# Four graph layers in one kernel: another copy and product order in the edge loops of layers 2 and 3, narrower node products, other scatter shares

## The chip, the cores and the metric

The kernel runs on one core of one Trainium2 chip. The metric is the device time of one execution in microseconds. Engines are called PE (matrix products), DVE, ACT, POOL and SP; each takes its own list of instructions in order and waits on semaphores (counters) for the others. PEld is the loading of a product's stationary operand, which overlaps PE. DMAs are issued from the queues of SP, ACT and POOL.

## What is computed

Four layers of message passing (l = 0 to 3) over N = 6250 nodes with 160 features each (64 scalars and 32 vectors of three) and E = 100000 edges. Each layer adds to the node features. The reference, cut to the pattern of one layer (l = 0; the others differ in widths, in the activation, and l = 2 also has a cross product and gates its output):

```python
h = jnp.maximum(_layernorm(x, axis=-1), 0.0)
x0, x1 = _split(h)                                   # 64, 32x3
s0, s1 = _fctp_scalar_attr(x0, x1, z, W_sc0, W_sc1)  # skip rows
h0, h1 = _fctp_scalar_attr(x0, x1, z, W_l1_0, W_l1_1)
w = jax.nn.silu(edge_features @ W_fc1 / np.sqrt(NEF)) @ W_fc2 / np.sqrt(RN)
...
e0, e1 = h0[edge_src], h1[edge_src]
m0a = w0 * e0 * y0
m0b = w3 * jnp.einsum('eui,ei->eu', e1, y1) / np.sqrt(3.0)
m1a = (w1 * e0)[:, :, None] * y1[:, None, :]
m1b = w2[:, :, None] * (e1 * y0[:, :, None])
ns = jax.ops.segment_sum(mid_s, edge_dst, num_segments=N) * inv
nv = jax.ops.segment_sum(mid_v, edge_dst, num_segments=N) * inv
o0, o1 = _fctp_scalar_attr(ns, nv, z, W_l2_0, W_l2_1)
...
x = x + jnp.concatenate([c_s * s0 + c_x * o0, (c_s * s1 + c_x * o1).reshape(N, -1)], axis=1)
```

The last layer weighs skip rows and sums with the cosine and sine of an angle, itself a product of the sums.

## The kernel before

**Data.** Nodes lie in NB = 51 tiles of BN = 123. Edges are sorted by the tile of the node that they add to and padded, so that a group of GE = 512 edges (G = 4 columns of 128 partitions) adds to one tile; there are 208 groups in a layer, as 26 rounds of the loop variable i with eight groups u each. Edge tables TA (36 columns, for l = 0, 1, 3) and TB (72 columns, l = 2) lie in DRAM. TB is built by POOL, by indirect DMAs that scatter rows (L566): 2 x 200 of its 782 columns inside the edge loops of l = 0 and 1, the rest in three shares, BCH[0] of 174 columns before l = 0 and two of 104 between l = 0 and 1 and between 1 and 2.

**An edge stage** (one per layer) works group by group, two groups (u, u + 1) to a step, and the order on each engine is written out by hand:
- SP loads the group's table rows (L459, `load`).
- POOL gathers the node rows HT of the source nodes, four indirect DMAs a group (L647, `gather`).
- PE transposes the edge features (`tfeat`, L829, L834, L839), ACT copies them out (`edge_e`, L1058, L1060, L1062), PE multiplies by the first weights (`edge_f1`, called F1, L850, L854, L857), ACT applies the activation (`edge_s`, L1072, L1075), PE multiplies by the second weights (`edge_f2`, F2, L867, L872).
- DVE builds the one-hot matrix OH (L1538) and the messages from F2's result and the gathered rows (L1547 to L1568; for l = 2 L1575 to L1600), the last of which raises semaphore M. In l = 2 ACT makes a copy of two of three products for the cross product (L1091); in every layer it makes twelve scalings (L1096, `edge_n`, semaphore N).
- PE multiplies the messages with OH (`edge_a`, A, L884), and DVE adds the result to the tile's sums ACC (L1509, semaphore V).

PE's order for a pair of groups is F1(u+2), F1(u+3), F2(u+2), A(u), transposes (u+4), (u+5), F2(u+3), A(u+1) (L907 to L914). ACT's is the two feature copies (u+2), (u+3), then scalings and activations in turn (L1101 to L1111). For l other than 2, DVE also splits the features of a later group into three bf16 parts in a ring XS of four buffers, four groups ahead (`parts`). Semaphores M and N of a layer start at 4 (L1317, L947), so that a loop's first rounds wait on positive numbers.

**A node stage** is `phase(lo, ln)` on every engine: it ends layer lo and begins layer ln, 51 tiles in turn. PE: the output product `mout` of the sums (L781), then, LAG = 10 tiles later, transposes (`tnode`, L735 to L740) and node linear (`mnode`, L751 to L761). ACT: normalised rows (`hid_`, L965), copying out the linear (`evac`, L976), clearing the sums (`clear`, L996), and the stores of HT and of the skip rows SC (`store`, L383, L386; for ln = 3 these are issued by SP). DVE: the new x (L1414) and the statistics of its layer norm. `mout` has nch = 3 products (4 for l = 2), one for each chunk of 128 (120) rows of the sums, all with the full output width: 160, 320 (as 2 x 160), 192 and 161 columns. Many of these columns have only zero weights for a given chunk. The node linear of l = 2 is four products.

After the last edge loop `phase(3, None)` computes the angles and the outputs, and puts them out in waves of tiles, LASTB.

## Time and profile before

| | |
|---|---|
| median of 3 runs | 5998.29 us (5996.16 to 6000.24) |
| the profiled execution | 5996.94 us, span 5994.8 us |
| PE busy | 4832.2 us, 81% of the span |
| PE weight loads | 4213.6 us, 70% |
| DVE busy | 4676.4 us, 78% |
| POOL busy | 4130.4 us, 69% |
| ACT busy | 3728.3 us, 62% |
| mean granted clock of PE | 0.953 |

The stages, as cut from the timeline, in us from the start of the span: preparation and the nodes of l = 0 to 453; edges of l = 0 to 1768; nodes 0 to 1 until 1903; edges of l = 1 to 3226; nodes 1 to 2 until 3422; edges of l = 2 to 4648; nodes 2 to 3 until 4855; edges of l = 3 to 5912; the last outputs to 5995. A busy share says how much of the time an engine had work, not that its work set the pace. The list of waits gives, for an engine and line, the idle time ahead of it and the instruction whose end is taken to have released it; "issue" there means idle time without a visible wait. An ended wait costs time only where the engine's next work is what the rest waits for.

### The profile page before, as it was taken

Reading aid. Unit: us, or ns where it says so; the run is one execution under the profiler, and the core shown is the slowest. Engines: PE = TensorE matmul, PEld = TensorE weight load, DVE = VectorE, ACT = ScalarE, POOL = GpSimd, SP = SyncE. Lnnn points to the kernel's source line nnn. Section 1 sums busy time; section 2 is a strip of 40 time slices with the busy share of each in tenths; the row PEclk is TensorE's granted clock in tenths of the full one; section 3 lists DMA queues with packets and bytes.
Section 4 is the critical chain, followed back from the end, with each engine's and each line's share of the span. In section 5 each row is a group of like instructions: output and inputs, shape, how many; then the busy total and the mean of one; then the engine's idle time right before and its main releaser. Section 6 shows DMA issues by size and latency. Waiting matters only on the chain. (4 is left out here: it accounts for less than half of the span.)

```text
span 5994.8 us, 143106 instructions
## 1 busy us (share of the span) xinstructions
PE 4832.2 (81%) x37237; PEld 4213.6 (70%) x37237; DVE 4676.4 (78%) x14209; ACT 3728.3 (62%) x12996; POOL 4130.4 (69%) x4263
## 2 busy tenths in 40 slices
PE   0078787777888888888889899999999778888886
PEld 0047777777777777777777688888888657777776
DVE  9947777777777777777776499999998569999996
ACT  0046666666665666666665477777777567777774
POOL 1677777777777777777777377777776257777773
PEclk9999999999998999999999899999999879999998
DMA  6433333333333333333333233333333223333332
GB/s 196 112 83 73 75 75 75 75 76 75 75 81 80 75 75 75 76 75 75 74 82 76 81 81 82 81 80 82 81 81 73 73 71 84 83 84 84 82 79 63
DMA packets 599359, 487.97 MB, mean 81 GB/s; under 512 B 308216, under 2 KB 525558, under 8 KB 598871
## 3 DMA queue, kind: packets, MB, share of 16 engines
q0 software_dynamic: 195056, 322.11, 21.0%
q1 hardware_dynamic: 365562, 137.46, 10.1%
q10 hardware_dynamic: 38637, 27.25, 1.5%
q8 instruction: 37, 0.61, 0.0%
q14 instruction: 67, 0.55, 0.0%
HBM read 410.36 MB, written 75.56 MB: 81 GB/s over the span
## 5 line engine op out<-in xcount | busy, mean ns | idle before, releaser
L884 PE MATMUL PS<-WK 128*128 128x123 f32 (+1 forms) x21632 | 2714.0, 285 | 196.8 <-issue 190.0
L884 PEld LDWEIGHTS PS<-WK 128*128 128x128 f32 (+1 forms) x21632 | 2598.1, 198 | 357.9 <-issue 349.2
L1096 ACT ACTIVATE WK<-WK 128x64 f32<-128x64 f32 x9984 | 2468.7, 334 | 352.1 <-DVE WK L1550 351.5
L647 POOL DMA_INDIRECT WK<-HT,WK x2080 | 2032.4, 977 | 797.7 <-issue 706.6
L647 POOL DMA_INDIRECT ACC<-HT,WK x832 | 795.8, 957 | 253.4 <-issue 242.7
L566 POOL DMA_INDIRECT TB<-WK x718 | 720.1, 1003 | 248.3 <-issue 230.7
L1072 ACT ACTIVATE WK<-PS 100x512 f32<-100x512 f32 x420 | 247.0, 588 | 693.3 <-PE PS L850 693.2
L867 PE MATMUL PS<-F,WK 100*128 100x192 f32 x3360 | 657.6, 340 | 11.2 <-DVE WK L1568 8.8
L872 PE MATMUL PS<-F,WK 64*128 64x224 f32 (+1 forms) x3360 | 416.3, 367 | 214.6 <-ACT WK L1075 214.6
L867 PEld LDWEIGHTS PS<-F,WK 100*128 100x128 f32 x3360 | 541.4, 192 | 66.5 <-DVE WK L1568 37.4
L1538 DVE SCALAR_TENSOR_TENSOR WK<-iota,BKOA,WK 128x492 f32<-128x492 f32 x624 | 453.3, 726 | 156.8 <-PE PS L884 107.6
L647 POOL DMA_INDIRECT WOA<-HT,WK x416 | 435.6, 1047 | 172.9 <-issue 118.3
L872 PEld LDWEIGHTS PS<-F,WK 64*128 64x128 f32 x3360 | 280.6, 189 | 317.0 <-issue 305.3
L1547 DVE TENSOR_TENSOR WK<-WK 128x384 f32<-128x384 f32 x416 | 232.6, 559 | 343.5 <-DMA WK<-HT,WK 340.7
L1509 DVE TENSOR_TENSOR ACC<-ACC,PS 128x369 f32 (+1 forms) x832 | 474.5, 570 | 0.0
L1547 DVE TENSOR_TENSOR WK<-ACC,WK 128x384 f32<-128x384 f32 x208 | 116.2, 559 | 308.5 <-DMA ACC<-HT,WK 308.5
L1075 ACT ACTIVATE WK<-PS 64x256 f32<-64x256 f32 x840 | 316.1, 376 | 55.7 <-PE PS L854 45.4
L1058 ACT ACTIVATE WK<-PS 72x512 bf16<-72x512 bf16 (+1 forms) x420 | 225.6, 586 | 113.4 <-PE PS L829 108.6
L850 PE MATMUL PS<-WK,FB 72*100 72x512 bf16 (+1 forms) x420 | 166.8, 397 | 157.7 <-issue 152.7
L829 PE MATMUL PS<-identb,WK 128*72 128x128 bf16 (+1 forms) x1696 | 154.5, 223 | 150.9 <-DVE WK L1487 117.7
L1558 DVE TENSOR_TENSOR WK<-PS,WK 128x256 f32<-128x256 f32 x624 | 261.8, 420 | 0.0
L829 PEld LDWEIGHTS PS<-identb,WK 128*72 128x72 bf16 (+1 forms) x1696 | 114.7, 112 | 180.8 <-issue 168.6
(234 smaller groups left out, 6605.7 us busy)
## 6 DMA issues: line engine op xcount, KB each, us to landing
WK<-TA SPq DMA_DIRECT2D x636, 72.0 KB, 1.9
WK<-HT,WK POOLq DMA_INDIRECT x2080
WK<-TB SPq DMA_DIRECT2D x212, 144.0 KB
WK<-in_ea SPq DMA_DIRECT2D x23, 612.0 KB
TA<-WK POOLq DMA_DIRECT2D x23, 612.0 KB, 7.9
ACC<-HT,WK POOLq DMA_INDIRECT x832
WK<-in_eb SPq DMA_DIRECT2D x400, 32.0 KB
HT<-WK ACTq DMA_DIRECT2D x153, 76.9 KB
```

Of the source, the lines that this page charges most:

```text
L566: eng.indirect_dma_start(out=T[:, :], out_offset=bass.IndirectOffsetOnAxis(ap=ps(q), axis=0), in_=st[:, q, :], in_offset=None).then_inc(sm ...
L647: eng.indirect_dma_start(out=GB[l][u % 4][:, t, :], out_offset=None, in_=HT[:, :], in_offset=bass.IndirectOffsetOnAxis(ap=idx[:, t, vc:vc ...
L829: m = eng.transpose(psT[k][0:6 * kf_, t * 128:(t + 1) * 128], x[:, t, 0:6 * kf_], identb[:, :])
L867: m = eng.matmul(psW[q][:, t, 0:wn], HH[l][q][0:hid, t * 128:(t + 1) * 128], F2[l][:, :], start=True, stop=True)
L872: m = eng.matmul(psW[q][:, a // 32 + t, 0:wn], HH[l][q][a:a + 64, t * 128:(t + 1) * 128], F2[l][a:a + 64, :], start=True, stop=True)
L884: m = eng.matmul(psA[q][0:ch, k * BN:(k + 1) * BN], ms[:, t, k * ch:(k + 1) * ch], OH[q][:, t, :], start=(t == 0), stop=(t == G - 1))
L1075: m = eng.activation(hh[a:a + 64, 0:256], psQ[q][a // 64][a:a + 64, :], p["fn"], scale=p["scale"])
L1096: m = eng.activation(m4[:, t, 96 + vb * c:160 + vb * c], m4[:, t, 96:160] if l == 2 else TW[l][q][:, t, :], ACT.Copy, scale=tb[:, t, y1 + ...
L1509: eng.tensor_tensor(acc[:, bass.ds(j, 1), :], acc[:, bass.ds(j, 1), :], psA[q][0:ch, 0:na].unsqueeze(1), ALU.add).then_inc(e.V, 1)
L1538: op(eng.scalar_tensor_tensor(out=OH[q], in0=iota1[:, :].unsqueeze(1).to_broadcast([128, G, BN]), scalar=BKO[b][:, bass.ds(i * 8 + (u + 2) ...
L1547: kp = op(eng.tensor_tensor(tp[q], e1, y1b.to_broadcast([128, G, 3, 32]), ALU.mult))
L1558: op(eng.tensor_tensor(m4[:, :, 0:64], W[:, :, 0:64], ty, ALU.mult))
```

## The change

Layers count from 0 in the code; the "layer 3" of the change is l = 2 in the order of the edge loop (which l = 3 takes over as well), and l = 2 for the node linear.

- **Edge loops of l = 2 and 3.** Everything up to the activation runs two groups further ahead: PE's order for a pair becomes F2(u+2), A(u), F2(u+3), transposes (u+6), (u+7), F1(u+4), F1(u+5), A(u+1). ACT's becomes the copy for u (`edge_w`, l = 2), the activations (u+2), (u+3), the scalings of u, the copy for u + 1, the feature copies (u+4), (u+5), the scalings of u + 1. What opens and ends the loops follows. In l = 3 DVE splits features six groups ahead instead of four, and the table rows have one semaphore a group (`landed`) instead of one a pair. M and N start at 8.
- **Output products.** `fed(l, k)` gives the columns that the rows of chunk k feed; the products run over these alone. Chunk 0 comes first and covers all.
- **Node linear of l = 2.** Two products instead of four: the weights WS2 get 32 columns of zeros, and the results go to the same places with strides.
- **Scatters.** The shares become 166, 96 and 120 columns.

```diff
-SB0, SB1 = 174, 104
+SB0, SB1, SB2 = 166, 96, 120
 NT0 = 25
 HC = EC // 2
 SLOOP = NT0 * 8
 
 
 NMIN, NMAX = 26, 31
-assert SB0 + 2 * SLOOP + 2 * SB1 == EC and EC % CHA == 0
+assert SB0 + 2 * SLOOP + SB1 + SB2 == EC and EC % CHA == 0
 BLK, LAG = 4, 10
...
 
 
-BCH = [chunks(0, SB0), chunks(SB0 + SLOOP, SB1), chunks(SB0 + 2 * SLOOP + SB1, SB1)]
+BCH = [chunks(0, SB0), chunks(SB0 + SLOOP, SB1), chunks(SB0 + 2 * SLOOP + SB1, SB2)]
 BL0 = [SB0, SB0 + SLOOP + SB1]
...
-        WS = [sb("WS0", [64, 128]), sb("WS1", [128, 128]), sb("WS2", [64, 160]), sb("WS3", [64, 128])]
+        WS = [sb("WS0", [64, 128]), sb("WS1", [128, 128]), sb("WS2", [64, 192]), sb("WS3", [64, 128])]
...
+                self.one = l == 3
+                self.L = [sem(f"e{l}_L{i}") for i in range(8 if l == 3 else 4)]
                 self.G = [sem(f"e{l}_G{i}") for i in range(4)]
                 self.T, self.E, self.F1, self.S, self.F2, self.M, self.A, self.V, self.D, self.N = (
                     sem(f"e{l}_{n}") for n in ("T", "E", "F1", "S", "F2", "M", "A", "V", "D", "N"))
+
+            def landed(self, eng, g, i):
+                if self.one:
+                    eng.wait_ge(self.L[g % 8], i * 16 + 16 * (g // 8 + 1))
+                else:
+                    eng.wait_ge(self.L[g % 8 // 2], i * 32 + 32 * (g // 8 + 1))
...
             loads += [(RW[a], w[f"L1_gnn_Ws_l2_{s}"]), (RW[2 + a], w[f"L1_gnn_Wv_l2_{s}"])]
         loads += [(RW3s, w["L1_gnn_Ws_l3"]), (RW3v, w["L1_gnn_Wv_l3"])]
-        loads += [(WS[2][:, 0:64], w["L2_gnn_W_nl0"]), (WS[2][:, 64:160], w["L2_gnn_W_skip0"])]
+        loads += [(WS[2][:, 0:64], w["L2_gnn_W_nl0"]), (WS[2][:, 96:192], w["L2_gnn_W_skip0"])]
...
+        def fed(l, k):
+
+            p, ns = LAYERS[l], 96 if l == 2 else 64
+            if k == 0:
+                return 0, 161 if l == 3 else ns + 96
+            blocks = [(0, 96, 0, ns)] + [(96 + c * p["vb"], p["vb"], ns + 32 * c, 32) for c in range(3)]
+            hit = [(c, c + n) for f, m, c, n in blocks if f < (k + 1) * p["ch"] and k * p["ch"] < f + m]
+            return hit[0][0], hit[-1][1]
+
...
 
                 def load(i, u):
-                    k = i * 8 if i is n else i * 8 + (u - 3)
-                    eng.wait_ge(e.M, 4 if isinstance(i, int) else k)
-                    eng.wait_ge(e.N, 4 if isinstance(i, int) else k)
+                    k = i * 8 + (u + 1)
+                    eng.wait_ge(e.M, 8 if isinstance(i, int) else k)
+                    eng.wait_ge(e.N, 8 if isinstance(i, int) else k)
                     r = eng.value_load(TI[b][32:33, bass.ds(i * 8 + (u + 2), 1)], min_val=0, max_val=EPAD)
-                    eng.dma_start(TT[l][u], T[bass.ds(r, GE), :].rearrange("(p t) f -> p (t f)", t=G)).then_inc(e.L[u // 2], 16)
+                    eng.dma_start(TT[l][u], T[bass.ds(r, GE), :].rearrange("(p t) f -> p (t f)", t=G)).then_inc(e.L[u if l == 3 else u // 2], 16)
...
                     idx = TT[l][u].rearrange("p (t f) -> p t f", t=G)
-                    eng.wait_ge(e.L[u // 2], i * 32 + 32)
-                    eng.wait_ge(e.M, i * 8 + (u + 1))
+                    e.landed(eng, u, i)
+                    eng.wait_ge(e.M, i * 8 + (u + 5))
...
                     if ln == 2:
-                        eng.matmul(o[:, 0:64], t[0:64, 0, 0:BN], WS[2][:, 0:64], start=True, stop=True)
-                        eng.matmul(o[:, 160:256], t[0:64, 0, 0:BN], WS[2][:, 64:160], start=True, stop=True)
-                        eng.matmul(o[:, 64:160], t[0:96, 1, 0:BN], KV[2][:, 0:96], start=True, stop=True)
-                        m = eng.matmul(o[:, 256:352], t[0:96, 1, 0:BN], KV[2][:, 96:192], start=True, stop=True)
+                        s2 = o[:, 0:320].rearrange("p (a f) -> p a f", a=2)[:, :, 0:96]
+                        v2 = o[:, 64:448].rearrange("p (a f) -> p a f", a=2)[:, :, 0:96]
+                        eng.matmul(s2, t[0:64, 0, 0:BN], WS[2][:, :], start=True, stop=True)
+                        m = eng.matmul(v2, t[0:96, 1, 0:BN], KV[2][:, :], start=True, stop=True)
                     else:
                         v = o[:, 0:320].rearrange("p (a f) -> p a f", a=2)
...
                             eng.wait_ge(s_xo, base + j - 3)
-                    nc_ = WO[lo].shape[2]
                     for k in range(nch):
-                        m = eng.matmul(psO[j % 4][0:BN, 0:nc_], acc[:, j, k, :], WO[lo][:, k, :],
-                                       start=(k == 0), stop=(k == nch - 1))
+                        c0, c1 = fed(lo, k)
+                        if lo == 1:
+                            o = psO[j % 4][0:BN, 0:320].rearrange("p (a f) -> p a f", a=2)[:, :, c0:c1]
+                            w_ = WO[1][:, k, :].rearrange("p (a f) -> p a f", a=2)[:, :, c0:c1]
+                        else:
+                            o, w_ = psO[j % 4][0:BN, c0:c1], WO[lo][:, k, c0:c1]
+                        m = eng.matmul(o, acc[:, j, k, :], w_, start=(k == 0), stop=(k == nch - 1))
                     m.then_inc(s_oo, 1)
 
...
                     elif not isinstance(i, int):
                         eng.wait_ge(e.D, i * (8 * ND[l]) + (u + 1) * ND[l])
                     elif g == 0:
                         eng.wait_ge(s_xp, min(l, 2) + 1)
+                    elif g == 4:
+                        eng.wait_ge(s_xp, 4)
                     if not isinstance(i, int) or g >= 2:
                         eng.wait_ge(e.E, i * 8 + (g - k))
-                        if l >= 2:
-                            eng.wait_ge(e.S, i * 8 + (g - k))
+                    if l >= 2 and (not isinstance(i, int) or g >= 4):
+                        eng.wait_ge(e.S, i * 8 + (g - k - 2))
                     eng.sem_inc(s_sep, 1)
                     x = XS[g % 4]
...
                     eng.wait_ge(e.S, i * 8 + (g + 1))
-                    eng.wait_ge(e.M, i * 8 + (g + 3))
+                    eng.wait_ge(e.M, i * 8 + (g + 7))
                     if l < 2:
                         for t in range(G):
...
                     ms = MS[l][q][:, 0:G * nm].rearrange("p (t f) -> p t f", t=G)
-                    eng.wait_ge(e.M, i * 8 + (u + 5))
-                    eng.wait_ge(e.N, i * 8 + (u + 5))
+                    eng.wait_ge(e.M, i * 8 + (u + 9))
+                    eng.wait_ge(e.N, i * 8 + (u + 9))
                     eng.wait_ge(e.V, i * 8 + (u + 2))
                     for k in range(nch):
...
-                edge_f1(0, 0, 0)
-                edge_f1(0, 1, 0)
-                tfeat(0, 2, 0)
-                tfeat(0, 3, 0)
+                if l < 2:
+                    edge_f1(0, 0, 0)
+                    edge_f1(0, 1, 0)
+                    tfeat(0, 2, 0)
+                    tfeat(0, 3, 0)
+                else:
+                    tfeat(0, 2, 0)
+                    tfeat(0, 3, 0)
+                    edge_f1(0, 0, 0)
+                    edge_f1(0, 1, 0)
+                    tfeat(0, 4, 0)
+                    tfeat(0, 5, 0)
+                    edge_f1(0, 2, 0)
+                    edge_f1(0, 3, 0)
                 edge_f2(0, 0, 0)
                 edge_f2(0, 1, 0)
 
...
-                        edge_f1(i, u, 2)
-                        edge_f1(i, u + 1, 2)
-                        edge_f2(i, u, 2)
-                        edge_a(i, u)
-                        tfeat(i, u, 4)
-                        tfeat(i, u + 1, 4)
-                        edge_f2(i, u + 1, 2)
-                        edge_a(i, u + 1)
-
-                eng.wait_ge(e.T, n * 8 + 4)
-                eng.wait_ge(e.F1, n * 8 + 2)
+                        if l < 2:
+                            edge_f1(i, u, 2)
+                            edge_f1(i, u + 1, 2)
+                            edge_f2(i, u, 2)
+                            edge_a(i, u)
+                            tfeat(i, u, 4)
+                            tfeat(i, u + 1, 4)
+                            edge_f2(i, u + 1, 2)
+                            edge_a(i, u + 1)
+                        else:
+                            edge_f2(i, u, 2)
+                            edge_a(i, u)
+                            edge_f2(i, u + 1, 2)
+                            tfeat(i, u, 6)
+                            tfeat(i, u + 1, 6)
+                            edge_f1(i, u, 4)
+                            edge_f1(i, u + 1, 4)
+                            edge_a(i, u + 1)
+
+                o = 2 if l >= 2 else 0
+                eng.wait_ge(e.T, n * 8 + (4 + o))
+                eng.wait_ge(e.F1, n * 8 + (2 + o))
...
-                    eng.wait_ge(e.F1, i * 8 + (g + 1))
+                    eng.wait_ge(e.F1, i * 8 + (g + 1 if l < 2 else g - q + 2))
                     if not (isinstance(i, int) and g < 2):
                         eng.wait_ge(e.F2, i * 8 + (g - 1))
...
-                edge_s(0, 0, 0)
-                edge_s(0, 0, 1)
+                if l < 2:
+                    edge_s(0, 0, 0)
+                    edge_s(0, 0, 1)
+                else:
+                    edge_s(0, 0, 0)
+                    edge_s(0, 0, 1)
+                    edge_e(0, 0, 2)
+                    edge_e(0, 0, 3)
+
+                def edge_w(i, u):
+
+                    eng.wait_ge(e.D, i * (8 * ND[l]) + (u * ND[l] + KW))
+                    eng.activation(tw[:, :, 3:5, :], tw[:, :, 0:2, :], ACT.Copy).then_inc(s_tw, 1)
+
                 def edge_n(i, u):
 
                     q = u % 2
                     R, y1 = (RB, SHC) if l == 2 else (RA, YC + 1)
                     tb = TT[l][u].rearrange("p (t f) -> p t f", t=G)
                     m4 = MS[l][q][:, 0:G * (96 + 3 * vb)].rearrange("p (t f) -> p t f", t=G)
-                    if l == 2:
-
-                        eng.wait_ge(e.D, i * (8 * ND[l]) + (u * ND[l] + KW))
-                        eng.activation(tw[:, :, 3:5, :], tw[:, :, 0:2, :], ACT.Copy).then_inc(s_tw, 1)
-                    else:
-                        eng.wait_ge(e.D, i * (8 * ND[l]) + (u * ND[l] + KT))
+                    eng.wait_ge(e.D, i * (8 * ND[l]) + (u * ND[l] + KT))
                     for t in range(G):
                         for c in (1, 2, 0):
...
-                        edge_e(i, u, 2)
-                        edge_e(i, u + 1, 2)
-                        if l >= 2:
+                        if l < 2:
+                            edge_e(i, u, 2)
+                            edge_e(i, u + 1, 2)
+                            edge_s(i, u, 2)
                             edge_n(i, u)
-                        edge_s(i, u, 2)
-                        if l < 2:
+                            edge_s(i, u + 1, 2)
+                        else:
+                            if l == 2:
+                                edge_w(i, u)
+                            edge_s(i, u, 2)
+                            edge_s(i, u + 1, 2)
                             edge_n(i, u)
-                        edge_s(i, u + 1, 2)
+                            if l == 2:
+                                edge_w(i, u + 1)
+                            edge_e(i, u, 4)
+                            edge_e(i, u + 1, 4)
                         edge_n(i, u + 1)
                 eng.wait_ge(s_le, l + 1)
 
...
                         w_()
-                    for u in range(4):
-                        eng.wait_ge(e.L[u // 2], 32)
+                    for u in range(4 if l < 2 else 6):
+                        if u == 4:
+                            eng.sem_inc(s_xp, 1)
+                        if u >= 4:
+                            eng.wait_ge(e.T, u - 3)
+                        e.landed(eng, u, 0)
                         x0, x1, x2 = parts(u)
                         for x in (x0, x1) + x2:
...
                             y0 = tb[:, :, yc:yc + 1]
-                            u4 = (u + 4) % 8
-                            x0, x1, x2 = parts(u4)
+                            ahead = 4 if l < 2 else 6
+                            x0, x1, x2 = parts((u + ahead) % 8)
                             kp = op(eng.tensor_tensor(tp[q], e1, y1b.to_broadcast([128, G, 3, 32]), ALU.mult))
                             eng.wait_ge(e.F2, i * 8 + (u + 1))
-                            eng.wait_ge(e.N, i * 8 + (u + 3))
+                            eng.wait_ge(e.N, i * 8 + (u + 7))
                             kt = op(eng.tensor_tensor(TW[l][q], W[:, :, 64:128], e0, ALU.mult))
                             assert kt == KT
...
-                            eng.wait_ge(e.L[u4 // 2], i * 32 + (32 * ((u + 4) // 8) + 32))
-                            eng.wait_ge(e.T, i * 8 + (u + 1))
+                            e.landed(eng, u + ahead, i)
+                            eng.wait_ge(e.T, i * 8 + (u + ahead - 3))
                             k0 = op(x0())
                             need(kr)
```

(The remaining lines move starting values and counts of semaphores with these: `sem_inc(EG[ln].M, 8)`, `sem_inc(EG[ln].N, 8)`, waits on M and N four higher, and some semaphores of the preparation that are merged into one.)

## Rows read from the trace of the kernel before

**Rows 1.** Windows by stage: us, busy (count) of PE, PEld, DVE, ACT, POOL; clock; DMA share; GB/s.
```profile
1768.00:1903.00 135.00, 119.26 (x800) 111.01 (x801) 105.22 (x463) 68.78 (x174) 98.01 (x100) 0.92 0.37 86
1808.00:1828.00 20.00, 20.00 (x145) 19.14 (x145) 18.59 (x84) 10.02 (x27) 15.43 (x16) 1.00 0.43 101
3226.00:3422.00 196.00, 177.73 (x873) 129.14 (x874) 81.78 (x346) 77.32 (x176) 92.85 (x98) 0.87 0.32 85
3422.00:4648.00 1226.00, 1165.98 (x10820) 1001.78 (x10818) 1128.19 (x2498) 907.98 (x3326) 863.01 (x824) 1.00 0.31 80
4648.00:4855.00 207.00, 147.77 (x748) 123.55 (x750) 97.52 (x465) 97.45 (x201) 50.19 (x66) 0.78 0.26 70
4855.00:5912.00 1057.00, 898.60 (x7912) 781.68 (x7910) 955.27 (x3121) 832.44 (x3118) 788.77 (x824) 0.96 0.34 81
```

**Rows 2.** Waits, 3422 to 4648 us: engine, line <- releaser: us, times, longest.
```profile
PE PS L872 <- ACT WK L1075: 58.5, 104, 5.8
```

**Rows 3.** Timeline, l = 2: start, us, engine, line, operation, [idle before <- releaser].
```profile
4011.80 3.65 PE L884 MATMUL PS<-WK 128*120 128x123 f32 x32
4015.38 1.08 PE L854 MATMUL PS<-WK,F 64*64 64x256 f32 x8
4016.97 1.03 PE L872 MATMUL PS<-F,WK 64*128 64x224 f32 x8 [0.51 <-ACT WK L1075]
...
4021.51 1.09 PE L834 MATMUL PS<-ident,WK 128*64 128x128 f32 x16
4022.53 1.03 PE L872 MATMUL PS<-F,WK 64*128 64x224 f32 x8
...
4015.59 0.73 DVE L1538 SCALAR_TENSOR_TENSOR WK<-iota,BKOB,WK 128x492 f32<-128x492 f32 x1
...
4019.89 0.55 DVE L1600 TENSOR_TENSOR WK<-WK 128x384 f32<-128x384 f32 x1
...
4016.07 1.56 ACT L1075 ACTIVATE WK<-PS 64x256 f32<-64x256 f32 x4 [0.42 <-PE PS L854]
4017.88 0.42 ACT L1091 ACTIVATE WK<-WK 128x256 f32<-128x256 f32 x1 [0.24 <-DVE WK L1580]
4018.20 2.96 ACT L1096 ACTIVATE WK<-WK 128x64 f32<-128x64 f32 x12
```

**Rows 4.** Waits, 4855 to 5912 us (the edge stage of l = 3).
```profile
POOL WK L647 <- issue: 231.8, 761, 0.3
...
POOL WK L647 <- PE PS L903: 3.1, 1, 3.1
```

**Rows 5.** Timeline, PE and its weight loads, between l = 0 and 1, then 1 and 2.
```profile
1802.87 0.98 PE L781 MATMUL PS<-WOA,ACC 128*123 128x160 f32 x6
...
3302.26 1.80 PE L781 MATMUL PS<-WOA,ACC 128*123 128x320 f32 x6
...
3304.20 0.29 PEld L751 LDWEIGHTS PS<-WS,WK 64*123 64x123 f32 x2 [0.17 <-issue]
...
3304.41 0.29 PEld L752 LDWEIGHTS PS<-WS,WK 64*123 64x123 f32 x2
...
3305.30 1.80 PE L781 MATMUL PS<-WOA,ACC 128*123 128x320 f32 x6
```

**Rows 6.** Timeline, stores being issued: ACT's queue from 1 to 2, SP's from 2 to 3.
```profile
3305.27 1.23 ACTq L383 DMA_DIRECT2D HT<-WK  x1
...
3306.53 1.91 ACTq L386 DMA_DIRECT2D SC<-WK  x1
...
4831.48 1.15 SPq L386 DMA_DIRECT2D SC<-WK  x1
```

**Rows 7.** Timeline, DVE in the last stage.
```profile
5921.17 0.17 DVE L1373 TENSOR_TENSOR ANG<-WK,ZZ 123x7 f32<-123x7 f32 x1 [8.40 <-ACT WK L1002]
```

**Rows 8.** Timeline, DVE before the first edge loop; waits, 3226 to 3422 us.
```profile
439.06 0.23 DVE L1484 CAST WK<-WK 128x144 bf16<-128x144 f32 x1 [16.90 <-ACT ACC L1043]
...
POOL WK L647 <- issue: 73.8, 8, 71.6
```

44 lines of the change are left out of this document (23 added, 21 removed).

## The prediction

> **What bounds the kernel now.** I read the stages first, since the whole-run shares (PE 81%, DVE 78%, POOL 69%) average over stages with different limits. Four edge stages (208 groups of 512 edges each) alternate with node stages. The first two edge loops get no changed instruction, so I read only the others [rows 1]. "l" counts layers from 0, so the change's "layer 3" is l = 2 and its neighbours.
>
> In the edge stage of l = 2 PE works 1166 of 1226 us, and the list of waits names one hole in it: the F2 product (L872) waits for ACT's activation (L1075) 104 times, 58.5 us in all, once per pair of groups [rows 1, 2]. In order of time, one pair on PE is: A 3.58 (11.80 to 15.38), F1 and its wait for ACT 1.59 (to 16.97), F2 0.96 and A 3.58 (together to 21.51), the transposes 1.02 (to 22.53), F2 0.96: 11.69 us [rows 3]. 104 such pairs are 1216 of the stage's 1226 us.
>
> In l = 3 the list of waits says something else: POOL pauses 0.30 us before nearly each gather and hardly for anything else [rows 4], and its 824 recorded instructions take 788.77/824 = 0.96 each [rows 1]. 832 gathers of 1.26 us are 1048 of 1057 us. That loop is bound by POOL's issuing.
>
> In the node stages PE is nearly always busy from l = 0 to 1 (20.00 of 20 us, with DVE at 18.59), and busy 178 of 196 us from 1 to 2, where a node takes 3.04 (3302.26 to 3305.30, from one L781 to the next) [rows 1, 5]. From 2 to 3 its mean clock is only 0.78 and other things end the waits [rows 1].
>
> **The change part by part.**
>
> *Narrower output products (L781).* Six instructions of 160 columns take 0.98 us and six of 320 take 1.80 [rows 5]: 0.82/(6 x 160) = 0.85 ns per column and instruction. A floor is seen beside it: two weight loads of 123 columns follow each other in 0.21 us although their products have only 64 columns, 0.105 each [rows 5]. So narrowing below about 123 columns buys nothing. Each product is two instructions. Layer 0 goes from 3 x 160 to 160, 64, 64: 4 x 37 x 0.85 ns = 0.13 us a node. Layer 1 from 3 x 320 to 320, 128, 128: 4 x 192 x 0.85 = 0.65. Layer 2 from 4 x 192 to 192, 64, 64, 32: 6 x 69 x 0.85 = 0.35. Layer 3 as layer 0. Times 51 nodes this is 7, 33, 18 and 7 us of PE.
>
> *Two products for the node linear of l = 2.* Four take 1.10 us (3304.20 to 3305.30) [rows 5]. Two of 192 columns are four instructions of 192 x 0.85 = 0.16 and two starts of about 0.15, 0.95 in all: 0.15 a node.
>
> What of this is on the path:
> - 0 to 1: DVE's 18.59 of 20 us allows 7% of some 80 us, so 6 at most where PE's share is 7. I take **-5** (bounds -7 and -2). POOL's scatters, shortened by 8 here, must end first; else they would be next.
> - 1 to 2: PE's 3.04 us a node become 2.24, but each node also has two stores issued from ACT's queue, and these take 1.23 and 1.91 us to issue while ACT's next work stands behind them [rows 6]: 3.1 us, as long as PE's node. This queue is late next. Without the row loads of SP, SP's stores of the next stage show 1.15 an issue, about 2.4 a node [rows 6]. The stage has 51 nodes; at 3.1 until the row loads end (about 60% of it) nothing is won, after that up to 0.6 a node, about 20 x 0.6 = 12, and about 4 in the first ten nodes, which have no stores. Against this the table loads of l = 2, which follow the scatters, come 16 x 1.26 = 20 us later (a scatter costs what a gather does: 92.85/98 = 0.95 busy [rows 1] and, as I take it, the same pause) and so into these last stores. I take **-5**, bounds +5 and -25 (all 51 nodes at 2.4).
> - 2 to 3: SP issues two stores a node, 2.4 us [rows 6], as long as PE's whole node now. PE's 18 us are hidden by them; only the start gains. **-1**, bounds -5 and +10.
> - The last stage: DVE idles 8.40 us until the first seven outputs are through [rows 7]; later it is DVE that has work. A quarter of these 8.40 goes: **-2**, bounds -4 and +10.
>
> *Scatters shared out anew.* 8 fewer before l = 0: DVE's wait there ends with ACT's clear of the accumulator (16.90 us of waiting for it [rows 8]), so 8 x 1.26 us of POOL's time gain **0**. If that cover were gone they would be worth 10. 16 more from 1 to 2 take 20 us of POOL, which idles 71.6 us there before its first gather [rows 8]: **0**.
>
> *The order in the edge loop of l = 2.* This is the large item on paper: F1 now runs a pair ahead, so the wait of 58.5 us for ACT cannot occur. What is late next? The new PE order is F2(u+2), A(u), F2(u+3), transposes (u+6, u+7), F1(u+4, u+5), A(u+1). F2(u+3) waits for DVE's messages of group u+1 (semaphore M), and behind it on PE now stand the transposes and F1, which before were done while DVE worked. That closes a loop: A(u-1) starts, DVE starts u+1 after it (4011.80 to 4015.59, 3.79 us), finishes its messages 4.85 us later (4020.44), then F2 0.96, transposes 1.02, F1, A(u+1) [rows 3]. F1 before another product is not in the trace: its eight instructions last 1.08, the transposes last 1.09 and give way after 1.02, so I take 1.01 (bounds 0.85 and 1.2). With 0.07 of signalling: 3.79 + 4.85 + 0.07 + 0.96 + 1.02 + 1.01 = **11.70 us a pair**, against 11.69 now. ACT closes a second loop: its two activations (1.56 together) now stand between the copy and the twelve scalings, so group u's scalings end 2.29 (the copy's start, 15.59 to 17.88) + 0.32 + 1.56 + 2.96 = 7.1 us after DVE starts u [rows 3], and A(u) waits for them. A(u), F2, transposes, F1 and A(u+1) until DVE may start u+3 add 3.58 + 0.96 + 1.02 + 1.01 + 3.79, the next group 5.5: 23.0 for two pairs, 11.5 each. Below the first, so it doesn't decide. Item: 104 x 0.01 = **+1**, bounds 104 x (11.54 - 11.69) = -16 and 104 x 0.2 = +21. PE alone would need 2 x 3.58 + 2 x 0.96 + 1.02 + 1.01 = 11.1, DVE 1128/104 = 10.85 [rows 1]; see the rival. The longer prologue (copy, F1 of groups 2 and 3 before F2 of group 0) delays the first group by about 2 us, of which the earlier first A gives back one: **+1**.
>
> *The same order in l = 3.* The gathers bound it. Its own loop as above is shorter than POOL's 8 x 1.26 = 10.1 a pair (A, F2 and F1 are shorter), and what PE no longer waits for falls on an engine with time to spare (busy 899 of 1057 us [rows 1]). Only the start changes, where POOL waits 3.1 us for the opening products [rows 4]: **-1**, bounds -4 and +3. The copy of 6 pieces ahead rather than 4 has its table rows loaded long before; landing by tile instead of by pair costs nothing.
>
> *Sum:* -5 - 5 - 1 - 2 + 0 + 1 + 1 - 1 = -12 us on the profiled execution's 5996.94 (span 5994.8 and 2.1 around it), 5985. The median of the runs is 1.35 us above that execution, within their spread. **Forecast 5985 us.**
>
> **The rivals.**
> - *The hole simply closes.* If PE, once rid of ACT, goes at its own 11.1 us a pair, l = 2 gains 104 x 0.55 = 57 us instead of losing 2: 5927. For it: PE is the busiest engine there. Against it: the first loop above is made of durations that stand in the rows, and nothing in the change takes its DVE part away.
> - *The stores don't bind from 1 to 2.* If the long issues are only the queue filling at PE's pace, the stage gains up to 25: 5965. For it: PE is busy 178 of the 196 us [rows 1]; against it: the two issues together are as long as the node, which needs no queue to explain it.
> - *The clock falls (slower).* From 2 to 3 the granted clock averages 0.78, and 1.00 in the dense 20 us of 0 to 1 [rows 1]; PE is given gaps by this change in each node stage. At 1.2 GHz a node of 1 to 2 costs PE about 4.1 us instead of 2.24, 1.0 more than today. It decides from the point where 13 nodes run so (13 us eat the gain); at half of the two middle stages it costs 27: 6012. The Trainium skill ("TensorE: Matmul & The Clock Gate", "Part 1: The HAM clock gate") has the array throttled by default and released by activity, so it speaks against thinning PE's work; by it alone this case would be the one to expect. The edge loops, which have gaps too, run at 0.96 and 1.00 [rows 1].
> - *Nothing is on the path:* the node stages wait for stores and DVE throughout, and l = 2 stays as it is: 5997.
>
> The Trainium skill ("DMA: Bandwidth & Descriptors", "Why a DMA increments its semaphore by 16 and not by 1") lets a transfer use as many engines as divide its row count, which for 123 rows is three; that fits the stores' long issues, which no row explains, and speaks for stores as the next bound.
>
> **How the numbers follow.** Forecast case 0.52, with its own range 5972 to 6000 (l = 2 from -16 to +21 in the main); closed hole 0.12; stores free 0.14; clock 0.14; nothing 0.08. A measurement of this kernel tells about 0.2%, 12 us, from no change. Of the forecast case 0.28 falls below 5986 and 0.24 inside 12 us; both gaining rivals count as faster, the clock as slower, the last as same: faster 0.54, same 0.32, slower 0.14. The range 5945 to 6010 leaves out most of the closed hole and about half of the clock case.
>
> **What would show it.** In l = 2: PE's wait for L1075 gone, in its place waits of L872 for DVE's L1600 and of L884 for ACT's L1096, the pair at 11.6 to 11.8. In l = 3: POOL still 1.26 a gather. From 1 to 2: L781 near 1.1 us for six, stores still 2.4 to 3.1 us a node. I am wrong if the pair of l = 2 falls under 11.4, if the stage from 1 to 2 shrinks by over 15 us, or if L781's weight loads go under 0.1 us apart.

## The result, and the profile after

The changed kernel takes **6036.14 us** (median of 4 runs, 6032.48 to 6038.70), the kernel before 5997.23 beside it: a ratio of 1.0062 with a 95% interval of 1.005 to 1.0075. It is 0.6% slower, where 5985 us and a gain were forecast, and it lies outside the range of 5945 to 6010. The profiled execution took 6038.70 us with a span of 6036.9.

The stages of both profiled executions, cut at the first output product and at the first opening product (L903, after the change L939) of each stage:

| stage | before, us | after, us | difference | forecast |
|---|---|---|---|---|
| preparation, nodes of l = 0 | 453.1 | 452.9 | -0.2 | 0 |
| edges l = 0 | 1315.2 | 1317.4 | +2.3 | 0 |
| nodes 0 to 1 | 134.2 | 130.4 | -3.8 | -5 |
| edges l = 1 | 1323.8 | 1328.6 | +4.8 | 0 |
| nodes 1 to 2 | 195.3 | 193.0 | -2.4 | -5 + 1 |
| edges l = 2 | 1227.1 | 1228.9 | +1.8 | +1 |
| **nodes 2 to 3** | 206.6 | 233.8 | **+27.2** | -1 |
| edges l = 3 | 1057.7 | 1052.2 | -5.5 | -1 |
| **last outputs** | 81.8 | 99.8 | **+18.0** | -2 |

Seven of nine stages came within 5 us of their terms, the edge loop of l = 2 with all its new order among them. The whole loss lies in two stages whose PE got less to do. The windows of those stages in the changed kernel, with columns as in [rows 1]: start and end; us; busy and count of PE, PEld, DVE, ACT, POOL; granted clock; DMA share; GB/s. A clock of 1.00 is 2.4 GHz, one of 0.50 is 1.2 GHz. The first line is the first 5 us of the stage.

```profile
4651.20:4656.20 5.00, 5.00 (x30) 5.00 (x31) 0.00 (x0) 1.11 (x1) 2.71 (x2) 0.72 0.17 48
...
4651.00:4885.00 234.00, 198.51 (x762) 165.40 (x762) 98.36 (x472) 100.46 (x203) 50.26 (x66) 0.51 0.23 62
4690.00:4720.00 30.00, 30.00 (x113) 25.40 (x112) 14.41 (x70) 15.74 (x32) 6.58 (x9) 0.50 0.25 65
4720.00:4860.00 140.00, 140.00 (x505) 114.50 (x503) 63.76 (x310) 67.99 (x138) 22.89 (x35) 0.50 0.22 63
...
5935.00:6036.00 101.00, 69.59 (x306) 69.44 (x306) 43.75 (x154) 16.21 (x56) 3.85 (x1) 0.51 0.18 51
```

The same places of the kernel before:

```profile
4648.70:4653.70 5.00, 4.99 (x31) 5.00 (x32) 0.00 (x0) 1.15 (x1) 2.68 (x2) 1.00 0.12 33
...
4690.00:4720.00 30.00, 30.00 (x170) 25.58 (x170) 21.43 (x105) 21.61 (x45) 8.61 (x13) 0.98 0.33 89
...
5912.00:5995.00 83.00, 43.92 (x306) 43.70 (x306) 43.30 (x153) 16.71 (x56) 3.85 (x1) 0.77 0.22 61
```

In both kernels PE is busy for all of the 30 us from 4690, but before it does 170 products there at a clock of 0.98, and after only 113 at 0.50, though each now has fewer columns. Then PE works 140 of 140 us without a gap at a clock of 0.50. In the last stage PE's 306 products take 69.6 us instead of 43.9.

Both kernels pause in this stage: after the first four nodes' output products PE waits 16 us for the skip rows, and the clock is 0.50 when it goes on. With the full width it comes back: in the kernel before it is 1.00 from 4694 to 4728 us, falls after a second pause at 4755 us and is 1.00 again by 4780. With the narrow products it does not come back in this stage. It is already lower ahead of the first pause, 0.72 against 1.00 in the first 5 us, in which PE is busy throughout in both kernels.

One node of the stage from 2 to 3 on PE, before and then after:

```profile
4710.50 0.27 PE L739 MATMUL PS<-ident,WK 123*64 123x123 f32 x1
...
4711.21 0.59 PE L763 MATMUL PS<-KV,WK 96*123 96x192 f32 x2
4711.64 1.47 PE L781 MATMUL PS<-WO,ACC 120*123 120x192 f32 x8
4712.94 0.27 PE L739 MATMUL PS<-ident,WK 123*64 123x123 f32 x1
```

```profile
4720.95 0.39 PE L759 MATMUL PS<-ident,WK 123*64 123x123 f32 x1
...
4722.20 1.00 PE L783 MATMUL PS<-KV,WK 96*123 96x192 f32 x2
4722.99 1.93 PE L806 MATMUL PS<-WO,ACC 120*123 120x192 f32 x8
4724.73 0.39 PE L759 MATMUL PS<-ident,WK 123*64 123x123 f32 x1
```

The operations that nobody changed show the clock: L783 is L763 of before and takes 1.00 instead of 0.59. The eight output products take 1.93 us instead of 1.47 in spite of 352 columns a pass instead of 768.

The Trainium skill ("TensorE: Matmul & The Clock Gate", "Part 1: The HAM clock gate") calls the throttled state the default, which activity releases. This trace agrees on the two levels (0.50 and 1.00), but not on "activity", if one reads that as PE having instructions: 140 us without a gap released nothing.

**The edge loop of l = 2** has the pair that was forecast. PE in the changed kernel:

```profile
4011.26 1.03 PE L898 MATMUL PS<-F,WK 64*128 64x224 f32 x8 [0.29 <-DVE WK L1665]
4012.21 1.09 PE L860 MATMUL PS<-ident,WK 128*64 128x128 f32 x16
4013.24 1.08 PE L880 MATMUL PS<-WK,F 64*64 64x256 f32 x8
4014.25 3.65 PE L910 MATMUL PS<-WK 128*120 128x123 f32 x32
4017.83 1.03 PE L898 MATMUL PS<-F,WK 64*128 64x224 f32 x8
4019.03 3.62 PE L910 MATMUL PS<-WK 128*120 128x123 f32 x32 [0.17 <-issue]
4022.95 1.03 PE L898 MATMUL PS<-F,WK 64*128 64x224 f32 x8 [0.30 <-DVE WK L1665]
```

From F2 (L898) at 4011.26 to F2 at 4022.95 is 11.69 us, as before [rows 3]; the product behind F1 (L880) starts 1.01 us after it. The waits of that stage (engine, line waited for, releaser: us, times, longest):

```profile
DVE WK L1603 <- PE PS L910: 91.7, 104, 3.4
...
PEld PS L898 <- DVE WK L1665: 50.1, 104, 6.2
...
PE PS L898 <- DVE WK L1665: 28.7, 79, 5.4
...
PE PS L910 <- ACT WK L1150: 9.9, 25, 0.6
```

The wait for L1075 [rows 2] is gone. In its place F2 or its weight load waits for DVE's last message (L1665) in every pair, and DVE waits for A to end (L910) in every pair: the loop that the forecast closed.

### The profile page after: what moved, and what is told of

It reads as the page before. It is cut to its first block and busy times, and to the rows that moved or that the text cites. A ratio compares the mean times of both kernels' runs of the same rounds, so it can differ in the third digit from the quotient of the medians.

```text
span 6036.9 us, 143521 instructions
## 1 busy us (share of the span) xinstructions
PE 4852.7 (80%) x37069; PEld 4220.0 (70%) x37069; DVE 4668.0 (77%) x14217; ACT 3745.6 (62%) x13000; POOL 4126.4 (68%) x4264
## 5 line engine op out<-in xcount | busy, mean ns | idle before, releaser
L910 PE MATMUL PS<-WK 128*128 128x123 f32 (+1 forms) x21632 | 2683.6, 283 | 263.6 <-issue 201.4
L910 PEld LDWEIGHTS PS<-WK 128*128 128x128 f32 (+1 forms) x21632 | 2571.9, 197 | 441.8 <-issue 409.8
L667 POOL DMA_INDIRECT WK<-HT,WK x2080 | 2029.2, 976 | 776.9 <-issue 670.0
L667 POOL DMA_INDIRECT ACC<-HT,WK x832 | 800.0, 962 | 253.5 <-issue 243.7
L898 PE MATMUL PS<-F,WK 64*128 64x224 f32 (+1 forms) x3360 | 412.0, 364 | 165.2 <-DVE WK L1633 135.2
L667 POOL DMA_INDIRECT WOA<-HT,WK x416 | 425.7, 1023 | 169.4 <-issue 117.4
L898 PEld LDWEIGHTS PS<-F,WK 64*128 64x128 f32 x3360 | 276.9, 187 | 237.3 <-DVE WK L1633 172.6
L1139 ACT ACTIVATE WK<-WK 128x256 f32<-128x256 f32 x208 | 86.7, 417 | 301.8 <-DVE WK L1645 301.8
```

What stands on the lines that cost most here:

```text
L667: eng.indirect_dma_start(out=GB[l][u % 4][:, t, :], out_offset=None, in_=HT[:, :], in_offset=bass.IndirectOffsetOnAxis(ap=idx[:, t, vc:vc ...
L898: m = eng.matmul(psW[q][:, a // 32 + t, 0:wn], HH[l][q][a:a + 64, t * 128:(t + 1) * 128], F2[l][a:a + 64, :], start=True, stop=True)
L910: m = eng.matmul(psA[q][0:ch, k * BN:(k + 1) * BN], ms[:, t, k * ch:(k + 1) * ch], OH[q][:, t, :], start=(t == 0), stop=(t == G - 1))
```

## The experiments

The times of the kernel before beside them are 5996.01 us (15 runs) for the first four and 5993.93 (13 runs) for g6 and g5. Theory A says that the narrow products keep PE at 1.2 GHz; theory B, that the new order does it by the way in which the edge loops end. Four stages of every kernel that ran on the chip where the kernel before takes 5990 to 6000 us, in us, each from one profiled execution:

| kernel | ratio (95%) | 1 to 2 | edges l = 2 | 2 to 3 | last |
|---|---|---|---|---|---|
| before | | 195.3 | 1227.1 | 206.6 | 81.8 |
| changed | 1.0062 (1.005 to 1.0075) | 193.0 | 1228.9 | 233.8 | 99.8 |
| e1_wide_23 | 0.9997 (0.9988 to 1.0006) | 191.6 | 1229.2 | 207.5 | 81.6 |
| e2_before_narrow | 1.0039 (1.0025 to 1.0053) | 184.5 | 1226.6 | 233.9 | 99.1 |
| e3_filled | 1.0073 (1.0057 to 1.0088) | 191.4 | 1229.4 | 233.7 | 99.8 |
| g6_width_128 | 0.9983 (0.9972 to 0.9994) | 191.4 | 1228.3 | 209.9 | 80.1 |
| e4_f2_last | 0.9958 (0.9944 to 0.9971) | 192.8 | 1208.7 | 205.5 | 80.1 |
| g5_act_first | 0.9894 (0.9878 to 0.9911) | 193.1 | 1167.1 | 205.9 | 81.6 |

**e1_wide_23**, full width again in layers 2 and 3:

```diff
-            if k == 0:
+            if k == 0 or l >= 2:
                 return 0, 161 if l == 3 else ns + 96
```

> The changed kernel with its output products (mout) of layers 2 and 3 back at full width (4 x 192 and 3 x 161 columns); layers 0 and 1 stay narrow, all else as changed. Theory A: the narrow products alone keep PE at 1.2 GHz in the node stage from 2 to 3 and in the last stage (there the profile shows a clock of 0.50 with PE busy without a gap). Then the stage from 2 to 3 goes from 233.8 back to 205 to 210 us, the last from 99.7 back to 80 to 84, and the whole from 6036 to about 5991. Theory B: the new order leaves the edge loops with a PE that idles before their end, so the node stages start at the low clock whatever their products. Then both stages stay within 5 us and the whole at 6031 to 6038.

Measured: 5993.23 us, with both stages back. Theory B, by which they would have stayed, falls. With the clock back, the rest of the change is worth nothing measurable either (0.9997, 0.9988 to 1.0006), where the forecast had 9 us for it. The windows of its two stages show the clocks of before (0.78 in [rows 1], 0.77 above):

```profile
4653.00:4860.00 207.00, 150.06 (x762) 124.31 (x762) 98.77 (x472) 97.77 (x203) 50.19 (x66) 0.78 0.26 70
...
5914.00:5995.00 81.00, 43.80 (x306) 43.58 (x306) 42.76 (x152) 16.67 (x56) 3.85 (x1) 0.77 0.22 63
```

**e2_before_narrow**, the other half of the test: the kernel before, with `fed` and the loop over chunks of the changed kernel's `mout`, nothing else.

> The kernel before with nothing but the narrow output products, in all four layers. Theory A: the stage from 2 to 3 grows from 206.6 to about 234, the last from 81.8 to about 100, 0 to 1 shrinks by 4, 1 to 2 by 2 to 5: 6033 to 6042 in all. Theory B: 2 to 3 and the last stage stay as they were or shrink a little, the whole comes to 5985 to 5995.

Measured: both stages are as slow as in the changed kernel with no new order at all:

```profile
4639.00:4873.00 234.00, 198.34 (x750) 166.05 (x750) 96.63 (x464) 99.84 (x201) 50.22 (x66) 0.50 0.23 62
5933.00:6032.00 99.00, 68.79 (x306) 68.63 (x306) 42.83 (x152) 16.22 (x56) 3.85 (x1) 0.50 0.18 52
```

So the narrow products alone are the cause. Why they have this effect on the clock no run separates. The whole came out lower than expected in the median, 6017.66 us, with runs from 6012.77 to 6034.27; the profiled one is the longest. A spread of 21 us is of the size of the last stage's 17 to 18, which suggests that this stage is granted its clock in some executions and not in others. Only the profiled run has stages to look at, so for this kernel that stays open; other kernels show such a stage below.

**e3_filled**: is it the start that counts, or the work? 60 products fill the gap in which PE waits for the skip rows.

```diff
                 def mout(j):
                     base = lo * NB
+                    if lo == 2 and j == 4:
+                        for _ in range(60):
+                            eng.matmul(psA[0][:, 0:128], ident[:, :], ident[:, :], start=True, stop=True)
```

> The changed kernel with 60 products of 128 x 128, whose results nobody reads, on PE ahead of the fifth output product of the stage from 2 to 3, in the 16 us in which PE waits for the skip rows. Theory A1: the narrow products are too thin at any time, the clock falls soon after the fill, and the stage keeps 225 to 236 us. Theory A2: the clock only has to be high when the products begin and then stays so: the stage comes to 200 to 210 us, the whole to about 6008. In both the last stage, which is left as it is, keeps its 99 to 101 us.

Measured: the filled gap, the windows that follow, and below them the output products of the first five nodes after the gap.

```profile
4665.00:4680.00 15.00, 15.00 (x123) 14.87 (x122) 0.00 (x0) 0.00 (x0) 3.56 (x5) 0.91 0.46 114
4680.00:4690.00 10.00, 6.64 (x49) 6.33 (x48) 7.99 (x36) 4.62 (x10) 2.54 (x5) 0.91 0.08 23
4690.00:4700.00 10.00, 7.36 (x29) 6.14 (x29) 7.64 (x37) 7.06 (x15) 3.97 (x4) 0.50 0.17 33
4700.00:4780.00 80.00, 80.00 (x296) 67.95 (x297) 37.99 (x185) 38.99 (x78) 16.84 (x24) 0.50 0.25 69
```

```profile
4681.03 5.06 PE L809 MATMUL PS<-WO,ACC 120*123 120x192 f32 x40 [0.97 <-DVE WK L1487]
```

The fill raised the clock (0.91 in the gap, where the changed kernel shows 0.50), and the narrow products began at the high clock: 5.06 us for five nodes, 1.01 each instead of 1.93. Ten us later it was 0.50, after short waits of PE for DVE and ACT; it stayed there through the next 80 us without a gap. The stage took 233.7: theory A1. These waits alone don't explain it, for at full width (e1) the clock falls at the same place and comes back:

```profile
4692.90:4697.90 5.00, 5.00 (x17) 4.29 (x16) 1.36 (x6) 1.57 (x4) 0.51 (x1) 0.50 0.34 102
4697.90:4702.90 5.00, 5.00 (x28) 4.05 (x27) 4.13 (x21) 2.76 (x6) 1.01 (x2) 0.90 0.22 67
```

A warm start is no cure here, since the stage has pauses behind it; the products that follow a pause must get the clock back.

**g6_width_128**: the later products at 128 columns, over zero weights.

```diff
-            p, ns = LAYERS[l], 96 if l == 2 else 64
+            p, ns = dict(LAYERS[l], wide=192 if l == 2 else 161), 96 if l == 2 else 64
...
             hit = [(c, c + n) for f, m, c, n in blocks if f < (k + 1) * p["ch"] and k * p["ch"] < f + m]
+            if l >= 2:
+                c0 = min(hit[0][0], p["wide"] - 128)
+                return c0, c0 + 128
             return hit[0][0], hit[-1][1]
```

> The changed kernel with the second and later output products at 128 columns in layers 2 and 3 (192, 128, 128, 128 and 161, 128, 128), the columns added having zero weights. If the clock follows how much the products do between the weight loads (theory A), at least one of the two stages returns to the high clock (205 to 212 us, 80 to 86 us), and one that stays at 1.2 GHz is longer than with the narrow products (over 234 and over 100). If only the full width brings the clock back, both stay low and the whole is 6040 to 6060.

Measured: 5986.73 us, both stages back (209.9 and 80.1). The windows of both, and a node of the middle stage:

```profile
4648.00:4858.00 210.00, 138.57 (x763) 113.46 (x764) 98.40 (x472) 98.83 (x204) 50.19 (x66) 0.75 0.26 69
5909.00:5989.00 80.00, 38.34 (x306) 37.98 (x306) 42.55 (x152) 15.80 (x56) 3.85 (x1) 0.74 0.23 64
```

```profile
4722.28 0.27 PE L762 MATMUL PS<-ident,WK 123*64 123x123 f32 x1
...
4723.42 1.14 PE L809 MATMUL PS<-WO,ACC 120*123 120x192 f32 x8
4724.40 0.27 PE L762 MATMUL PS<-ident,WK 123*64 123x123 f32 x1
```

2.12 us a node at the high clock, against 2.44 at full width and 3.78 at the narrow one. Yet the stage is no shorter than with full width (207.5): PE is busy for 138.6 of its 210 us and waits for others, as the prediction said. Around 4740 us SP issues the first of a node's two stores every 2.4 to 3.0 us (4739.85, 4742.48, 4744.87, 4747.82), more than PE's 2.12, which agrees with the stores as what comes next; no run took them away in this stage. So the cheaper products bring nothing here even where the clock survives them.

**e4_f2_last** starts from e1_wide_23 and tests the loop of l = 2:

```diff
                             edge_f2(i, u, 2)
                             edge_a(i, u)
-                            edge_f2(i, u + 1, 2)
+                            if l == 3:
+                                edge_f2(i, u + 1, 2)
                             tfeat(i, u, 6)
                             tfeat(i, u + 1, 6)
                             edge_f1(i, u, 4)
                             edge_f1(i, u + 1, 4)
+                            if l == 2:
+                                edge_f2(i, u + 1, 2)
                             edge_a(i, u + 1)
```

> The kernel of e1_wide_23, and in l = 2 PE's order for a pair is F2(u+2), A(u), transposes, F1(u+4), F1(u+5), F2(u+3), A(u+1): F2(u+3), which waits for DVE's messages, goes behind the transposes and F1. Theory C: the pair of 11.7 us is set by the loop A, DVE's messages, F2, transposes, F1, A; with transposes and F1 out of it, PE's own 11.1 is next: pair 11.1 to 11.3, the stage of l = 2 from 1228.9 to 1165 to 1185 us, the whole some 50 us below e1_wide_23. Theory D: ACT's loop (copy, activations, scalings) or the wait of DVE for A is as late: pair 11.5 or more, gain under 20 us.

Measured: the loop of l = 2 shrinks by 20.5 us, to 1208.7, and the whole to 5970.79. The waits of F2 for DVE are gone but for one, which shows that the loop of theory C was real; but the gain is less than half of what theory C expected, at the edge of what theory D did. The next holder is seen in its trace:

```profile
4011.80 2.97 ACT L1153 ACTIVATE WK<-WK 128x64 f32<-128x64 f32 x12
...
4013.16 1.03 PE L898 MATMUL PS<-F,WK 64*128 64x224 f32 x8
4014.87 3.62 PE L910 MATMUL PS<-WK 128*120 128x123 f32 x32 [0.68 <-issue]
```

A (L910) was next after F2 at 4014.12 and began at 4014.87, just after ACT's scalings (L1153) ended at 4014.77. The list of waits of this stage names the scalings ahead of A 26 times, 21.0 us in all. Ahead of a group's scalings stand ACT's copy and, in one group of two, its activations, and ahead of the copy ACT idles for DVE, 1.40 us before the copy that follows (`[1.40 <-DVE WK L1648]`):

```profile
4021.02 0.42 ACT L1142 ACTIVATE WK<-WK 128x256 f32<-128x256 f32 x1 [1.40 <-DVE WK L1648]
```

**g5_act_first** takes the activations out of that chain:

```diff
                             if l == 2:
+                                edge_s(i, u, 2)
+                                edge_s(i, u + 1, 2)
                                 edge_w(i, u)
-                            edge_s(i, u, 2)
-                            edge_s(i, u + 1, 2)
+                            else:
+                                edge_s(i, u, 2)
+                                edge_s(i, u + 1, 2)
                             edge_n(i, u)
```

> The kernel of e4_f2_last, and in l = 2 ACT does its two activations (u+2), (u+3) ahead of the copy for u instead of between copy and scalings. Theory E: ACT's scalings are what is late in e4_f2_last (DVE start, 2.3 to the copy, 1.6 activations, 3.0 scalings, A); with the activations gone from that chain the pair falls from about 11.4 to 11.1 or 11.2: the stage of l = 2 from 1208.7 to 1180 to 1192 us, the whole near 5950. Rival F: DVE's start after A is the bound and the stage keeps over 1203 us.

Measured: the stage falls to 1167.1, the whole to **5932.67 us**. The pair is the one that theory E gave; stage and whole came out lower than its 1180 and 5950. Rival F falls: DVE's waits for A are down to 5.4 us in 26 places. Its window and a pair on PE:

```profile
3423.00:4590.00 1167.00, 1159.48 (x10822) 1001.89 (x10820) 1124.33 (x2498) 906.49 (x3328) 810.11 (x824) 1.00 0.34 84
```

```profile
4011.18 3.65 PE L910 MATMUL PS<-WK 128*120 128x123 f32 x32
4014.75 1.09 PE L860 MATMUL PS<-ident,WK 128*64 128x128 f32 x16
4015.78 1.08 PE L880 MATMUL PS<-WK,F 64*64 64x256 f32 x8
4016.79 1.03 PE L898 MATMUL PS<-F,WK 64*128 64x224 f32 x8
4017.75 3.65 PE L910 MATMUL PS<-WK 128*120 128x123 f32 x32
4021.33 1.03 PE L898 MATMUL PS<-F,WK 64*128 64x224 f32 x8
4022.28 1.96 PE L910 MATMUL PS<-WK 128*120 128x123 f32 x16
```

4022.28 - 4011.18 = 11.10 us a pair, PE busy 1159 of 1167: this is the "hole closed" rival's 11.1, reached by two further moves. It beats both kernels: 0.9894 of before (0.9878 to 0.9911).

**On other chips.** Twelve runs went to three other chips, called 14 (e5 to e8), 12 (f5 to f8) and 8 (g7 to g10) here. The kernel before takes 8846, 8844 and 8991 us there. In the kernels traced there the edge loops are 38 to 65% longer than on the chip of the comparison, the stages from 0 to 1 and 1 to 2 longer too. On chip 12 the profile shows idle times without a releaser on this core ("remote"), over 2000 us of them ahead of DVE's one-hot in each of the four traces. Against the kernel before on the same chip, the kernel of g5_act_first has 0.962 and 0.963 (chips 14 and 12), that of g6_width_128 0.970 and 0.971, and the changed kernel with the old shares 0.976 on both, but 1.018 on chip 8. No cause of this was found, and times of different chips aren't compared. Within one chip the node stages still say something:

| run (chip) | shares | 0 to 1 | 1 to 2 | 2 to 3 | last | edges l = 3 |
|---|---|---|---|---|---|---|
| f5_act_first, wide (12) | new | 208 | 274 | 210 | 82 | 1695 |
| f6_width_128 (12) | new | 212 | 276 | 206 | 80 | 1684 |
| f7_old_shares, narrow (12) | old | 224 | 255 | 235 | 96 | 1691 |
| f8_no_skip_store, narrow (12) | new | 208 | 249 | 230 | 100 | 1709 |
| g9_best, 128 columns (8) | old | 220 | 257 | 209 | 80 | 1725 |
| g7_old_shares, narrow (8) | old | 218 | 257 | 236 | 86 | 1734 |
| g8_no_skip_store, narrow (8) | new | 208 | 254 | 233 | 80 | 1751 |
| g10_three_gathers, narrow (8) | new | 208 | 276 | 236 | 83 | 1538 |

The stage from 2 to 3 is the same on all four chips: 230 to 236 us with narrow products, 205 to 210 with 128 columns or more. The last stage comes out anywhere from 80 to 100 with narrow products and always at 80 to 82 with wide ones. Its length goes with its mean clock: 80 us at 0.74 (g8), 83 at 0.71 (g10), 85 and 86 at 0.69 (e7, g7), 92 at 0.61 (e8), 96 at 0.56 (f7), 100 at 0.50 (f8). So with the same narrow products this stage gets its clock in some executions and in others late or not at all.

e5 to e8 and f5 to f8 are the same four kernels, those of g5_act_first, g6_width_128, g7_old_shares and g8_no_skip_store. First e5_act_first and f5_act_first:

> The kernel of e4_f2_last, and in l = 2 ACT does its two activations (u+2), (u+3) ahead of the copy for u instead of between copy and scalings, so in a time in which it idled for DVE (1.4 us before the copy in the trace of e4_f2_last, where A waits 0.7 us until the scalings end). Theory E: after F2's place, ACT's scalings are what is late in that kernel (DVE start, 2.3 to the copy, 1.6 activations, 3.0 scalings, A); with the activations gone from that chain the pair falls from about 11.4 to 11.1 or 11.2: the stage of l = 2 from 1208.7 to 1180 to 1192 us, the whole near 5950. Rival F: DVE's start after A is the bound (it waits for A 95 times there) and the stage keeps over 1203 us.

> The kernel of e4_f2_last, and in l = 2 ACT does its two activations (u+2), (u+3) ahead of the copy for u instead of between copy and scalings. Theory E: ACT's scalings are what is late in e4_f2_last (DVE start, 2.3 to the copy, 1.6 activations, 3.0 scalings, A); with the activations gone from that chain the pair falls from about 11.4 to 11.1 or 11.2: the stage of l = 2 from 1208.7 to 1180 to 1192 us, the whole near 5950. Rival F: DVE's start after A is the bound and the stage keeps over 1203 us.

Measured: 8510.74 and 8521.86 us against 8846.23 and 8844.05, ratios of 0.9616 and 0.9632; the expected times are for the chip of the comparison. Next e6_width_128 and f6_width_128:

> The changed kernel with the second and later output products at 128 columns in layers 2 and 3 (192, 128, 128, 128 and 161, 128, 128 instead of 192, 64, 64, 32 and 161, 64, 64), the columns added having zero weights. If the clock follows how much the products between the weight loads do (theory A), this lies between: at least one of the two stages returns to the high clock (205 to 212 us, 80 to 86 us), and a stage that stays at 1.2 GHz is longer than with narrow products (over 234 and over 100 us). If only the full width brings the clock back, both stay, and the whole is 6040 to 6060.

> The changed kernel with the second and later output products at 128 columns in layers 2 and 3 (192, 128, 128, 128 and 161, 128, 128), the columns added having zero weights. If the clock follows how much the products do between the weight loads (theory A), at least one of the two stages returns to the high clock (205 to 212 us, 80 to 86 us), and one that stays at 1.2 GHz is longer than with the narrow products (over 234 and over 100). If only the full width brings the clock back, both stay low and the whole is 6040 to 6060.

Measured: 8570.05 and 8583.64 us; both stages at the length of the high clock (210 and 80, 206 and 80). Next e7_old_shares and f7_old_shares:

> The changed kernel with the scatter shares of before (174, 104, 104 columns). The prediction put the 16 more scatters from 1 to 2 at nothing, as hidden. Theory G: they are not hidden, since the table rows of l = 2 and the stores come later by them: the stage from 1 to 2 goes from 193 to 184 to 187 us (as in the kernel before with narrow products, 184.5), the whole 6 to 8 us below the changed kernel. Theory H: they are hidden, and what that other kernel won has another cause: 1 to 2 stays at 191 to 194.

> The changed kernel with the scatter shares of before (174, 104, 104 columns). The prediction put the 16 more scatters from 1 to 2 at nothing, as hidden. Theory G: they are not hidden, since the table rows of l = 2 and the stores come later by them: the stage from 1 to 2 goes from 193 to 184 to 187 us (as in the kernel before with narrow products, 184.5), the whole 6 to 8 us below the changed kernel. Theory H: they are hidden: 1 to 2 stays at 191 to 194.

Measured: 8613.71 and 8617.46 us; 254 and 255 us from 1 to 2. Next e8_no_skip_store and f8_no_skip_store, one execution each:

> The changed kernel without the stores of the skip rows SC from 1 to 2 (one of the two stores of each node); the loads of those rows read 160 columns of HT instead. If the two store issues a node on ACT's queue are what holds this stage, it goes from 193 to 150 to 175 us (a node at PE's 2.24 or at DVE's). If not (clock, POOL's scatters, or the rows that come last), it stays above 185.

> The changed kernel without the stores of the skip rows SC from 1 to 2 (one of the two stores of each node); the loads of those rows read 160 columns of HT instead, so the outputs differ. If the two store issues a node on ACT's queue hold this stage, it goes from 193 to 150 to 175 us. If the clock, POOL's scatters or the rows that come last hold it, it stays above 185.

Measured: 8626.46 and 8619.24 us; 256 and 249 us from 1 to 2.

g7_old_shares is the changed kernel with `SB0, SB1, SB2 = 174, 104, 104`.

> The changed kernel with the scatter shares of before (174, 104, 104 columns). The prediction put the 16 more scatters from 1 to 2 at nothing, as hidden. Theory G: they are not hidden, since the table rows of l = 2 and the stores come later by them: the stage from 1 to 2 goes from 193 to 184 to 187 us, the whole 6 to 8 us below the changed kernel. Theory H: they are hidden: 1 to 2 stays at 191 to 194.

On these chips the new shares make 1 to 2 longer by 18 to 21 us (274 against 254 on chip 14, 274 and 276 against 255 on chip 12, 276 against 257 on chip 8) and 0 to 1 shorter by 10 to 16. So there the moved scatters are on the path of both stages. On the chip of the comparison this kernel wasn't run; the only kernel there with narrow products and old shares, e2_before_narrow, has 184.5 from 1 to 2, and the six with new shares 191.4 to 193.1. That agrees with theory G, but e2 differs in the node linear and the opening of l = 2 as well, so it isn't shown.

g8_no_skip_store stores no skip rows for l = 2 and loads 160 columns of HT in their place.

> The changed kernel without the stores of the skip rows SC from 1 to 2 (one of the two stores of each node); the loads of those rows read 160 columns of HT instead, so the outputs differ. If the two store issues a node on ACT's queue hold this stage, it goes from 193 to 150 to 175 us. If the clock, POOL's scatters or the rows that come last hold it, it stays above 185.

Beside kernels with the same shares the stage is 22 us shorter on chip 8 (254 against 276), 25 on chip 12 (249 against 274) and 18 on chip 14 (256 against 274): the stores are part of what holds it, not all of it. Each of these kernels ran once, and on those chips alone.

g10_three_gathers issues three gathers a group in l = 3 instead of four.

> The changed kernel with one of the four gathers of each group left out in l = 3 (its rows keep what was there, so the outputs differ). The prediction had this loop bound by POOL's issues, 1.26 us x 832. If so, the stage of l = 3 falls from 1052 until DVE is next (961 us busy in it: 955 to 1000). If the order of PE, ACT and DVE holds it at the same pair anyway, it stays above 1035.

208 gathers fewer shorten the loop by 196 us beside g7 (1538 against 1734), 0.94 us each; beside g9 and g8 it is 187 and 213. On that chip, then, the gathers are on the path of l = 3. Leaving them out takes away their data as well as their issue, so which of the two it is isn't separated. The numbers of the expectation are for the other chip and weren't reached or refuted there. Last g9_best:

> All that the runs speak for together: the kernel of g5_act_first with the products of g6_width_128 (128 columns in layers 2 and 3) and the scatter shares of before. By the stages seen: 1 to 2 some 7 us shorter (theory G: the moved scatters are on the path), the rest as in g5_act_first: 5924 to 5930. If the moved scatters cost nothing: 5930 to 5936.

g9 has all parts together; it ran only on chip 8 (1.0072 of before, but 0.990 of g7 beside it). Whether it beats g5 is open.

## Why the prediction was wrong, point by point

- **The cover of the narrow products (2 to 3, last stage) failed, and with it the sum.** The prediction priced them in time at the high clock and asked only which other engine would be late next. It put 18 and 7 us of PE as saved and mostly hidden, -1 and -2. Measured: +27.2 and +18.0 us. At the high clock narrower products are cheaper, as priced (1.01 us for a node's eight in e3, 1.47 less the 0.35 of the prediction would be 1.12), but every price of the sum had that clock in it, and the clock stayed at 0.50, where the eight take 1.93. The rival "the clock falls" named this mechanism and gave it 0.14, at 6012. Its sign was right; its place was wrong (it took half of both middle stages, but from 1 to 2 the clock averages 0.81 against 0.87 and the stage still gains), and it left out the last stage. Its reason ("PE is given gaps") was wrong for the stage from 2 to 3: both kernels have the pauses there after which the clock is low, and in the changed kernel it then stays low while PE has no gap at all.
- **What the row could have told.** From 2 to 3 the clock of before averages 0.78 [rows 1]. The prediction read this as "other things end the waits" and took it for slack. In slices of 5 us it is 1.00 in the dense stretches and 0.50 after its pauses and shorter waits (at 4664, 4760 and 4812 us): a stage that has to get its clock back several times. The mean alone does not warn: the last stage averages 0.77 before mostly because PE has nothing to do in its last 37 us (0.81, then 0.50 there), and from 1 to 2 narrower products got the clock back twice (1.00 from 3299 and from 3339 us).
- **l = 2: right.** 11.70 us a pair were worked out, 11.69 came; the stage +1.8 for +1. The two new waits are the ones that were named. e4 and g5 show that this was no accident: with F2 out of the loop the pair falls to the 11.5 worked out for ACT's loop (e4: F2 starts at 4013.16 and, two pairs later, at 4036.11), and with ACT's activations out of that one to PE's 11.1.
- **0 to 1: not borne out.** -3.8 came for -5 in the profiled execution, but of six other kernels with the same narrow products four have 134.2 to 134.4 there (the others 132.7 and 134.8), as long as before's 134.2. A gain of more than noise isn't shown.
- **1 to 2: the sum was near (-2.4 for -4), a term in it not.** The longer opening of l = 2 was put at +1: from the first transpose to the first opening product it is 14.3 us (3408.04 to 3422.31) where it was 11.0 (3410.62 to 3421.63), +3.3. While POOL scatters, the HT stores start 3.2 us apart in the mean (36 of them, 3254.3 to 3366.1), as before (3.3, 27 of them, 3252.2 to 3337.1), and PE's node fell from 3.04 to 2.22 us beside them:

```profile
3300.34 0.87 ACTq L399 DMA_DIRECT2D HT<-WK  x1
3303.54 1.58 ACTq L399 DMA_DIRECT2D HT<-WK  x1
...
3300.01 0.27 PE L759 MATMUL PS<-ident,WK 123*64 123x123 f32 x1
3302.23 0.27 PE L759 MATMUL PS<-ident,WK 123*64 123x123 f32 x1
```

  That the stores come next was right as far as these rows go. That the 16 scatters are free is doubtful (above): the last one starts at 3367.3 instead of 3339.2 us.
- **l = 3: right in kind.** POOL's waits (L667 <- issue, 231.6 us, 760 times) are those of [rows 4]. The stage is 5.5 us shorter for -1, and 1051 to 1054 in all kernels with the new order against 1057.7 and 1059.9 without it. By their starts the 832 gathers take 1047.9 us from first to last instead of 1054.3, so some of POOL's longer waits fell away; which part of the change did that isn't separated.
- **Edges of l = 0 and 1: +2.3 and +4.8** for 0, though no instruction in them changed. l = 0 takes 1317.4 to 1318.8 in all kernels with the new shares, and 1315.2 in both with the old; the cause is open. l = 1 takes 1324.0 to 1332.2 in the six kernels with the same code and shares there, so its +4.8 is spread.
- **Luck.** Apart from the two stages of the clock the terms of the sum add up to -9 and the stages to -3.0, with +7.1 from loops put at 0 and -5.5 from one put at -1. So seven of nine stages within 5 us of their terms does not mean seven terms that were right.

## What to carry to other kernels

Here the width of products decided not only their time but also whether PE got its clock back. Before narrowing products in a stage, look at its granted clock in slices of a few us: where it falls in a pause and comes back with the products behind it, narrower ones may leave it at 1.2 GHz, whatever PE's busy share says. The run with zero-weight columns up to 128 is the test for it. Where a wait in a hand-made order is removed, write down the loops through every engine and put the next one behind work that doesn't need it; here two such moves brought 62 us, and the removed wait alone had gained nothing. Test a bundle's parts apart: the slow part of this one cost 45 us (27.2 + 18.0) and hid an order that, with those two moves, shortens its loop from 1229.2 to 1167.1.

## What the runs showed of the hardware

- PE worked 140 us without a gap at a granted clock of 0.50 (changed kernel, 4720 to 4860 us), with products of 192, 64, 64 and 32 columns behind weight loads of 123; the same stage with 192, 128, 128 and 128 was granted 0.75 in the mean (g6), near the 0.78 of full width.
- 60 products of 128 columns raised the clock in the pause (0.91 in its mean, where the changed kernel shows 0.50), and five nodes of narrow products ran at the high clock behind them; after the next short waits it was 0.50 and stayed so for 80 us without a gap (e3).
- The last stage with the same narrow products took from 80 us at a mean clock of 0.74 to 100 at 0.50, with wide ones 80 to 82.
- Three of four chips ran the kernel before 47 to 50% slower (8844 to 8991 us); in the kernels traced there the stage from 2 to 3 has its usual length.
